# First experts' layer: SyncE asks for the rows of the next block ahead of the current block's biases, and ScalarE issues the stores

## The reference, cut to what matters

```
def _moe(tokens, router_w, w1, b1, w2, b2):
    logits = tokens.astype(jnp.float32) @ router_w.astype(jnp.float32).T
    probs = jax.nn.softmax(logits, axis=-1)
    rw, re = jax.lax.top_k(probs, TOP_K)
    rw = rw / jnp.maximum(rw.sum(-1, keepdims=True), 1e-12)
    combine = jnp.zeros((N, E), tokens.dtype).at[jnp.arange(N)[:, None], re].set(rw)
    out = tokens
    for e in range(E):
        h = jax.nn.gelu(tokens @ w1[e] + b1[e], approximate=False)
        y = h @ w2[e] + b2[e]
        out = out + combine[:, e:e + 1] * y
    return out
...
x = x + _L0_ffn_ref(_layernorm(x, axis=-1)[None], L0_ffn_router_w, ...)[0]
```

## Time and profile before

| | us |
|---|---|
| median of 3 runs (2792.14 to 2793.42) | 2792.26 |
| the profiled execution, its own time | 2789.74 |
| its span | 2787.7 |
| first mixture, first rows' request to the next layer's first DMA | 1406.01 to 1590.98 |

### The profile page before, as it was taken

One profiled execution on the slowest core, in us unless ns is written; L12 is line 12 of the kernel. 1 busy time (PEld: TensorE's weight loads), 2 busy tenths in 40 slices (PEclk: granted clock), 3 DMA queues, 4 the chain that ended last, 5 costly groups with the idle time before them and its releaser, 6 DMA issues. The chain is left out here.

```text
span 2787.7 us, 50123 instructions
## 1 busy us (share of the span) xinstructions
PE 2289.8 (82%) x10903; PEld 1803.5 (65%) x10904; DVE 1490.0 (53%) x2999; ACT 1246.7 (45%) x2511; POOL 716.6 (26%) x720
## 2 busy tenths in 40 slices
PE   1688876889989895997468399995999954999995
PEld 0344443666666663886456288884888853888884
DVE  7799975898888887332733644544002153111113
ACT  1799943777777772223223122343324431222221
POOL 0000011777777770000374311000110006002013
PEclk9999997999999998999589699997999956999998
DMA  5421222777777770000166322221222105656555
GB/s 196 200 76 73 76 82 81 208 212 213 212 212 212 213 203 20 22 0 4 49 212 193 109 76 70 69 67 53 67 67 74 55 2 189 218 191 221 189 204 178
DMA packets 183896, 353.28 MB, mean 127 GB/s; under 512 B 55346, under 2 KB 138727, under 8 KB 179111
## 3 DMA queue, kind: packets, MB, share of 16 engines
q1 hardware_dynamic: 138328, 206.94, 22.9%
q0 software_dynamic: 45520, 145.80, 18.1%
HBM read 275.32 MB, written 77.31 MB: 126 GB/s over the span
## 5 line engine op out<-in xcount | busy, mean ns | idle before, releaser
L2279 PE MATMUL gnn_p<-gnn_y,gnn_counts_wide 128*128 (+1 forms) x2500 | 553.6, 381 | 2.7 <-DVE R_kept L2161 2.6
L2279 PEld LDWEIGHTS gnn_p<-gnn_y,gnn_counts_wide 128*128 128x128 f32 x2500 | 473.1, 191 | 69.1 <-DVE R_kept L2161 6.6
L856 POOL DMA_INDIRECT kv_pair<-kv,gather_idx x448 | 428.1, 956 | 150.6 <-issue 103.6
L2084 ACT CAST gnn_counts_wide<-gnn_counts 128x1664 f32<-128x1664 uint16 x100 | 158.0, 1580 | 387.1 <-PE gnn_p L2279 368.0
L956 PE MATMUL p_edge_q<-QX_kept,onehot_turned 128*128 x904 | 264.1, 415 | 61.6 <-ACT onehot_turned L919 54.7
L1926 ACT ACTIVATE experts_hidden<-experts_p_hidden,experts_pack 128x256 f32<-128x256 f32 x290 | 134.1, 472 | 337.3 <-PE experts_p_hidden L1958 337.3
L1958 PE MATMUL experts_p_hidden<-experts_turned,experts_pack 128*128 128x256 f32 x1160 | 263.6, 383 | 2.1 <-DVE experts_turned L1857 1.2
L956 PEld LDWEIGHTS p_edge_q<-QX_kept,onehot_turned 128*128 128x128 f32 x904 | 155.4, 191 | 166.6 <-issue 151.1
L1967 PE MATMUL experts_p_y<-experts_pack,experts_hidden 128*128 128x256 f32 x1160 | 260.2, 379 | 0.0
L1958 PEld LDWEIGHTS experts_p_hidden<-experts_turned,experts_pack 128*128 128x128 f32 x1160 | 222.7, 192 | 33.6 <-issue 2.8
L964 PE MATMUL p_sums<-R_kept 128*128 128x264 f32 x896 | 237.3, 388 | 0.0
(11 more groups left out here) (376 smaller groups left out, 3214.2 us busy)
## 6 DMA issues: line engine op xcount, KB each, us to landing
experts_pack<-experts SPq DMA_DIRECT2D x29, 2052.0 KB, 8.8
gnn_counts<-adj SPq DMA_DIRECT2D x400, 104.0 KB, 2.2
adj<-adj_counts SPq DMA_DIRECT2D x100, 208.0 KB, 1.9
experts_rows<-slots_in SPq DMA_DIRECT2D x60, 256.0 KB, 3.8
slots_out<-experts_y SPq DMA_DIRECT2D x58, 256.0 KB, 7.7
experts_rest<-experts SPq DMA_DIRECT2D x60, 130.0 KB, 8.0
kv_pair<-kv,gather_idx POOLq DMA_INDIRECT x448, 3.8
slots_in<-R_kept SPq DMA_DIRECT2D x2, 3328.0 KB, 13.9
```

The costliest lines, as they stand in the source:

```text
L856: pool.indirect_dma_start(kv[r][:, j, :], None, a["kv"], bass.IndirectOffsetOnAxis(ap=idx[r][:, j:j + 1], axis=0)).then_inc(kv_in[r], 16)
L2084: act.copy(wide[b][:], raw[r][:].rearrange("p q s -> p (q s)")).then_inc(wide_ready, 1)
L2279: mm = pe.matmul(bank[:, off:off + D], wide[b][:, j * P:(j + 1) * P], y[:, at(n), :].squeeze(1), start=first and off == 0, stop=last and ( ...
```

## The change

For layer 0 only, SyncE runs another step, `light_step`. In step j it asks for the rows of block j+1, after the turn of block j-1, then waits for the bias addition of block j-2 and asks for the biases of block j. The rows of block 0 are asked ahead of the loop. It stores nothing, and it asks no longer for a set of biases that nobody uses. ScalarE stores the result of block j-1 behind the activations of block j, and the last block's behind its loop. Layer 1 keeps its code.

```diff
+            def light_step(j, b, i, first, last):
+                load_rows(j + 1, 1 - b, j)
+                _, e = block_of(nc, mybir.EngineType.SP, k, j)
+                if not first:
+                    sp.wait_ge(y_ready, j - 1)
+                    sp.sem_inc(tally, 1)
+                load_rest(e, b)
+
...
-            n = over_blocks(sp, step)
-            e = load_rows(2 * n + 1, 1, 2 * n)
-            store(2 * n - 1, 1, 2 * n)
-            load_rest(e, 1)
-            store(2 * n, 0, 2 * n + 1)
+            if layer:
+                n = over_blocks(sp, step)
+                e = load_rows(2 * n + 1, 1, 2 * n)
+                store(2 * n - 1, 1, 2 * n)
+                load_rest(e, 1)
+                store(2 * n, 0, 2 * n + 1)
+            else:
+                load_rows(0, 0, 0)
+                n = over_blocks(sp, light_step)
             for landed_, count in [(y_out[0], n + 1), (y_out[1], n), (rows_in[0], n + 1), (rows_in[1], n + 1),
-                                   (rest_in[0], n + 1), (rest_in[1], n + 1)]:
+                                   (rest_in[0], n + 1), (rest_in[1], n + 1 if layer else n)]:
...
                     act.activation(hid[b][:, h, :], pH[h % NH][:, 0:BT], ACT.Gelu,
                                    bias=pack[b][:, B1 + h:B1 + h + 1]).then_inc(gelu_done, 1)
+                if not layer and not (isinstance(j, int) and j == 0):
+                    store(j - 1, 1 - b, j)
+
+            def store(j, b, ready):
+                slot, _ = block_of(nc, mybir.EngineType.Activation, k, j)
+                act.wait_ge(y_ready, ready)
+                act.dma_start(slots_out[at(slot)].squeeze(0), y[b][:]).then_inc(y_out[b], 16)
...
-            over_blocks(act, step)
+            n = over_blocks(act, step)
+            if not layer:
+                store(2 * n, 0, 2 * n + 1)
```

## The result

The changed kernel takes 2772.11 us (median of 13 runs, 2770.62 to 2788.73), the kernel before 2790.9 (13 runs on the same chip, 2788.28 to 2808.16): ratio 0.9932, 95% interval 0.9918 to 0.9947, a gain of 19 us, give or take 4. Predicted were 2771.9 and a gain of 20.4.

The account below looks back on a forecast made before the run. Late row requests, through SyncE's order, held blocks at 4.79 us. 27 steps of 4.02 save 20.8, less 0.4 at loop entry: 20.4 off 2789.74, 2769.3; median 2.5 above, 2771.9 us; range 2768.5 to 2778.5.

Parts of the forecast that it names:

- The rows' wait goes entirely: TensorE's 28.7 us of waits for token rows vanish; rows asked one block ahead have 1.8 us or more of cover.
- ScalarE's loop is next, at 4.02: ScalarE's loop of weights copy, activations and hand-over to the product sets the next step: 4.02 us a block, before 4.79.
- The loop's entry, 0.4: Where ScalarE enters its loop, the weights copy stays late by 0.98 us instead of 0.56, costing 0.4 us.
- The stores cost ScalarE nothing: A store adds near 1.0 us on ScalarE, ending before the next product's end: 0 on the path, some 0.6 us cover.
- Later stores are harmless: Stores leave at about +2.9 us after their product and land by +7.2, before the buffer is written again at 8.2.
- DMA load: On the 16 DMA engines, hardware queue 52% and software queue some 28% at the new pace: 80%, no bound.
- The tail shifts as one: Gathers and additions after the last block keep their length: next layer starts 42.8 us after the last second product.
- Sum: 27 steps of 4.02 make 108.5 us against 129.3, 20.8 less; minus 0.4 at ScalarE's loop entry, gain 20.4 us.
- (a): ScalarE's queue becomes the bound: 2.06 us for a store, step 4.41, gain 10.3 us, 2782 us; chance 0.08.
- (b): Transfers overlap more and some waits stay, or `landed` holds an early one: step 4.2, 2777 us; chance 0.12.
- (c): Stores so slow that the y buffers bound: landing after 10 us gives a 5.7 us step, 2817 us; chance 0.03.
- (d): Rows still late because SyncE's requests are held by `y_ready`, the wait for additions: 2792 us; chance 0.02.

Follow-up runs that it names:

- the order alone: Against the changed kernel, SyncE keeps the stores, ahead of the biases, and still asks rows one block ahead: 3137.89 us, ratio 0.9978 to before, on a disturbed chip.
- the stores alone: Against the changed kernel, SyncE returns to its old request order while ScalarE stores: 3142.28 us disturbed; ordinary 2782.95 against 2790.36 of before, ratio 0.9965.
- the largest pad: Changed kernel plus a useless copy of 2.76 us on ScalarE behind each store: 2782.45 us beside 2792.25 of before, steps 4.46 on the mean.
- the copy behind: Changed kernel with ScalarE's copy of the next block's weights moved behind the two activations: ordinary 2766.41 us against 2790.36 of before, ratio 0.9916.
- the three pads: Changed kernel plus useless ScalarE copies behind each store: 1.05 us, ratio 0.9993 to before; 1.90 us, 0.9998; 2.76 us, 2782.45 us beside 2792.25.
- the later stores: Changed kernel with each store issued one block later, block j-2 behind the activations of block j: 3138.62 us, ratio 0.9991 to before, on a disturbed chip.

## Why the prediction was right, point by point

- *The rows' wait goes entirely.* Right. Asked at +3.1 and +3.39 in turns (said 3.3 to 3.7), 6.2 us or more ahead of the turn, no row in the waits. SyncE's step has time left, as said: it waits 22.0 us for the additions in 26 steps, 0.85 of 4.09 each. The stores had to leave its queue for that; with them its loop is 4.22 (the order alone). Undoing the earlier request (the stores alone) brings 19 waits back.
- *ScalarE's loop is next, at 4.02.* Right, and shown by taking the copy out of it: 3.89. Mis-sized as a mean: 4.087 was measured. Eighteen steps have 4.02 to 4.05; the nine of 4.08 to 4.39 exceed 4.03 by 1.47 us together, which is most of the 1.8 us that the sum of 27 steps missed. In these nine the copy starts 0.60 to 0.91 us behind the end of y, in the others 0.55 to 0.57, and the time goes into the table load that stands between the two in ScalarE's queue. Here are all of them, 1434 to 1546 (ns, minimum, median, maximum):

```profile
L430 ACTq TENSOR_LOAD <-ORDER x55: 274/284/637, 1435.6 to 1545.0; - x55
```

  Behind y it takes 280 to 291 ns in the eighteen steps and 327 to 637 in the nine, the 637 in the step of 4.39. In the earlier trace rows it was 273 to 284, and the sum had the copy at +0.56 in every step. Before has such loads of up to 697 ns as well (1420 to 1548), without any store on ScalarE; why single ones take longer is not shown.
- *The loop's entry, 0.4.* Smaller in its own place: behind the y of 1437.79 the copy is at +0.80 instead of 0.56, 0.24 us, and that is part of the 27 steps.
- *Ahead of block 1: at nothing.* The sum had no term for the piece from the first rows' request to y of block 1, and it took 14.07 us instead of 12.87. The first products run at the clock's lower level (1.2 GHz, granted 0.50), and the clock rose later behind the first turn, at which TensorE had waited 16.6 us for the rows (16.5 in before): some 7.6 us behind it here, 5.4 in before (0.50 in 1412:1414, 0.88 in 1414:1416, the turn at 1409.09). y of block 0 took 2.47 us for 1.89. The windows of after (columns as in the earlier trace rows), its turn at 1422.80:

```profile
1428.00:1430.00 2.00, 2.00 (x8) 1.66 (x7) 0.57 (x1) 0.47 (x1) 1.48 (x2) 0.50 0.43 157
1430.00:1434.00 4.00, 4.00 (x21) 3.51 (x20) 1.02 (x4) 1.78 (x3) 3.08 (x4) 0.96 0.56 173
```

  The same piece took 14.12 us in the kernel with the largest pad, where the clock rose 8.0 us behind the turn, and 12.76 in the one with the copy behind, 12.81 with the stores alone and 13.06 in before run again, where it rose 5.0 to 5.5 behind. Kernels with the rows asked ahead are on both sides, so nothing shows that the edit chooses the value.
- *The stores cost ScalarE nothing.* Right in result, and too cautious in size: ScalarE has 1.8 us free behind a store that ends at +2.74, where 0.6 were given behind one that ends at 3.3 to 3.4. The sum put the table load behind the two activations; it runs during them (from 1499.3, and the activations last until 1499.76). The store was mis-sized, though its 0 us stand.
- *Later stores are harmless.* Right: landed by +2.36 + 4.7 = 7.1 at the worst, and one block later still did no harm.
- *DMA load.* 0.73 of the engines' time in the blocks' stretch, said 0.80; no bound. Landings of rows grew by 1.1 us at the most.
- *The tail shifts as one.* Right: 42.60 us after the last second product, 42.8 before.
- *Sum.* Steps 19.00 (said 20.8 less 0.4), the piece ahead of block 1 -1.20 (said nothing), tail 0.16: 17.96 in the profiled stage, said 20.4. The medians differ by 18.8.
- *The time itself, 2771.9 against 2772.11,* is closer than the sum deserves, by luck: the gain was 1.6 us smaller than said, and before came out 1.4 us lower (2790.9) than the 2792.26 that the forecast started from.
- *Rivals.* (a) falls with the three pads (its sign, a copy later than 0.56 behind y, was there in nine steps, but through the table load and not the store), (b) is half seen (a mean step of 4.09, between 4.02 and 4.2, without waits for rows), (c) with the later stores, (d) with the waits.

How the gain divides: the stores alone bring two fifths to a half of it. The order alone takes the wait away, 4.02 a step over seven steps, but with SyncE's own loop at 4.22 it would not hold that; by the estimate above it brings all but 5.4 us or less. The two parts overlap, and neither is enough for 4.02 over the whole stage as far as is known; the order alone in an ordinary execution was not run.

## What to carry to other kernels

When an engine that only issues transfers is late with a request, look for how far ahead its buffer allows the request, and move that across the waits of other blocks' work; shortening what stands ahead of it helps only by its own length. Then compare the issuing engine's own loop with the step: a lead hides for a while that the engine is too slow (4.22 against 4.02 us here), and a short stretch of a trace does not show it unless the lead itself is read, block by block. Price an added DMA or table load on a computing engine by what its queue does while the engine computes, not in line with the computation. And ask at once which loop is next: here it was 3% above TensorE's floor (4.02 against 3.89 us), and moving three more lines took the rest.

## What the runs showed of the hardware that was not expected

**Queues that stand still.** On two chips (35 runs of before each, 3131 to 3164 us together) all kernels took 350 us more; on the first of them before took 2792.25 a quarter of an hour later. So this belongs to a time, not to a chip or a kernel. In the attention's edge phase (600 to 1000 us) the instructions of ScalarE's queue that compute a register, usually some 50 ns, take up to 0.7 us each (duration ns min/median/max). The disturbed execution of the change, then before once more, ordinary:

```profile
L908 ACTq FUSED_REGOPS  x333: 3/51/722, 600.3 to 999.6; - x167
```
```profile
L908 ACTq FUSED_REGOPS  x477: 37/51/90, 600.5 to 997.6; - x159
```

In the same 400 us, 333 of them ran instead of 477. It coincides with GpSimd's indirect DMAs: SyncE's table loads in the mixture take 700 ns (median) while GpSimd scatters, and 274 when it has nothing to issue.

```profile
L430 SPq TENSOR_LOAD <-ORDER x4: 16/700/702, 1653.7 to 1684.5; - x4
...
L430 SPq TENSOR_LOAD <-ORDER x16: 265/274/533, 1705.0 to 1735.9; - x16
```

GpSimd's gathers of results (1735.74 to 1744.54, and three more groups) each coincide with a gap in the steps. What causes it, and why only at some times, is open.

**A 15 us excess in single executions** of several kernels here; the two that were profiled (the change and the stores alone) have it in the same gathers (first section). It decides what a single profile shows, so totals were compared by medians and the stage by its own times.

**ScalarE's queue works beside its computation**: pads of 1.05 and 1.90 us and the store together cost nothing, and at 2.76 us the step is ScalarE's busy time and no more.
